# A top-k search split by batches: batches 0 and 1 searched ahead, expert 0's row groups by halves of the batches

## The chip, the cores and the metric

The kernel runs on 1 core of a Trainium2 chip. The metric is device microseconds (us) of one execution, as the median of several runs; lower is better. A profiled execution is a separate one, with its own time.

## The reference

`x` is (4, 1024, 256), the context (4, 64, 256), all in float32. A residual cross-attention comes first, then a residual mixture of 8 experts in which each expert chooses its tokens:

```python
x = x + xattn(layernorm(x), ctx, Wq, bq, Wk, bk, Wv, bv)   # scores without a scale, softmax over 64 keys
xn = layernorm(x)
probs = softmax(einsum('BTC,CE->BTE', xn, gate_w))
top_p, top_idx = top_k(transpose(probs, (0, 2, 1)), 256)    # per batch and expert, 256 of 1024 tokens
xin = xn at top_idx                                         # (4, 8, 256, 256)
h = gelu(einsum('BElC,ECH->BElH', xin, w1))                 # H = 1024
y = einsum('BElH,EHC->BElC', h, w2) * top_p
x = x + zeros.at[b, top_idx].add(y)
```

## The kernel before, in words

Each engine has its own program, written out by hand; semaphores are the only order between them. TensorE is PE, VectorE DVE, ScalarE ACT, GpSimd POOL, SyncE SP.

**Attention and gate.** The 32 chunks of 128 tokens are worked on in 8 groups of 4 (`NG`, `GT`). After a group DVE adds its attention (`x_all`, L1106) and SP stores the rows to the output. DVE and ACT make the gate's softmax `prob` in two halves, batches 0 and 1 (h=0) and batches 2 and 3 (h=1).

**Search.** The 256th largest probability of each batch and expert is found bit by bit, three bits a round, in 2 x 5 rounds (`ROUNDS`) for each half. A round of a half is a ring over two engines: DVE compares the keys with 7 candidates (`compare`, `over`, L1186, two instructions), PE counts (`count`, L872, 8 matmuls of one column), DVE tests the counts (`keep_reached`, L1192), PE turns the result into a new floor (`raise_floor`, L880), DVE makes the next candidates (`candidates`, L1197). `rounds` interleaves the two halves. Between rounds 4 and 5 the keys change from the upper to the lower 15 bits (`take_floor`, `above`, `with_lower`, `second_key`).

**First list.** For expert 0 `place_chosen(0, 0, 1)` marks the chosen tokens of all four batches and numbers them by a scan on DVE and two matmuls (`rank_bases`, L897 and L898), a one-hot product on PE (`list_expert`, L907) turns the numbers into row indices, and `index_list` writes them to `gidx`. Here a tile of 128 gathered rows holds 32 rows of each of the four batches.

**Rows in.** ACT normalises `x_all` in place (L655), SP stores it to `xn_rows` in DRAM (L447), and POOL gathers by indirect DMA, four tiles of 128 rows for each of two row groups (`gather`, L525). PE transposes the tiles (`turn`, L750), ACT rounds them (`xhi`), DVE takes the rest (`xlo`). For expert 0 the first two tiles of group 0 go ahead of the other two (`first_turn`, `first_ff1`, L994), with `keep_warm` transposes of no use before and between them.

**Expert loop.** An expert has 16 steps: 8 slices of H for row group 0, then 8 for row group 1. In a step s, PE does `ff1(s + 2)` (6 matmuls, L932) and `ff2(s)` (4 tiles, L949 and L953); ACT does the gelu (L689), DVE splits it (`split_h`, L1366 and L1368). Weights of the next expert are loaded by SP once `w2_split` shows that the raw buffers are free (L453, L454), and split by ACT and DVE from step 7 on (`w1_part`, `w1_rest`, L1374). Group 1 is turned at steps 1 and 2, the next expert's list is made at step 3 and its `gidx` at step 6, its group 0 is turned at steps 10 and 11. POOL scatters the results with an add (L533), one group after each gather. The first `ff2` of a group waits for `y_ready`, which DVE raises; for expert 0 that is a semaphore increment without work (`dve.sem_inc(y_ready, NL)`), and in the kernel before it stands ahead of `place_chosen(0, 0, 1)`. `ff1(2)` waits for the first gelu. Experts 0 to 6 run as a loop, expert 7 is written out.

Of the kernel before, what the change touches and what calls it, by code (L numbers as in the profile page):

```python
# [34 lines left out]
P = 128  # L35
# [10 lines left out]
def build(nc, x, xT, ctxT_in, Wq, WkT, Wv, WvT, bv, small, w1, w2, out):  # L46
# [33 lines left out]
    assert UB == HB and NU == 2  # L80
    assert KC == 2 and UT == 512 and B * S == 2 * P and NC * E == 256
# [8 lines left out]
    with ExitStack() as stack:  # L90
# [91 lines left out]
        own_tok = sb("own_tok", [P, NB, B], F32)  # L182
        sidx = sb("sidx", [P, NB], I32)
# [52 lines left out]
        rows_stored = sem("rows_stored")  # L236
        rows_added = sem("rows_added")
        settled = sem("settled")
        xn_stored = sem("xn_stored")
# [17 lines left out]
        all_found = sem("all_found")  # L257
        masks = sem("masks")
# [45 lines left out]
        N_CONST = 12  # L304
# [29 lines left out]
        def counts(h):  # L334

            return bank[h][:, 0:1]

        def floors(h):

            return bank[2 + h][:, 0:HB * E]  # L340

        def bases(i, n):

            return bank[2 + 2 * i][:, 0:n * 2 * B].rearrange("p (e m b) -> p e m b", e=n, m=2)
# [31 lines left out]
        def first_bank(k, rest):  # L376

            return bank[(2, 6)[k] + (1 if rest else 0)][:, 0:UF]

        def gathered_rows(g, e):  # L380

            return 16 * NL * (e + 1) - (16 * FIRST if g == 0 else 0)

# [21 lines left out]
        def _(sp):  # L405
# [23 lines left out]
            def store_rows(g):  # L429
                sp.wait_ge(x1_ready, GT * (g + 1))  # L430
                sp.dma_start(out_g[:, g // GB, g % GB], xcols(g)).then_inc(rows_stored, 16)
# [13 lines left out]
            for b in range(B):  # L445
                sp.wait_ge(xn2_ready, GB * (b + 1) + 1)
                sp.dma_start(xn_v[:, b], x_all[:, b]).then_inc(xn_stored, 16)  # L447
# [15 lines left out]
        def _(pool):  # L463
# [16 lines left out]
            pool.memset(go_on[:, :, :, :, 0:1], 0.0).then_inc(consts, 1)  # L480
            pool.iota(slot_no[:], [[1, SL], [0, TC]], base=0, channel_multiplier=0).then_inc(consts, 1)
# [55 lines left out]
            pool.wait_ge(own_set, 1)  # L537
# [5 lines left out]
            pool.wait_ge(xn_stored, 16 * B)  # L543
            pool.wait_ge(gidx_ready, 1)
            for g in range(NU):
                gather(g, FIRST if g == 0 else 0)

            def expert(e, last):
                if not last:
                    pool.wait_ge(gidx_ready, e + 2)  # L550
# [13 lines left out]
            pool.wait_ge(rows_stored, 16 * NG)  # L564
# [5 lines left out]
        def _(act):  # L570
# [76 lines left out]
            gate_exp(HALF, NC, 1)  # L647

            act.wait_ge(rows_stored, 16 * NG)
            act.wait_ge(nb2_ready, 1)  # L650

# [6 lines left out]
            for g in range(GB):  # L658
                normalise(g)
            act.wait_ge(normed, 6)  # L660
            act.activation(x_all[:, :, :, C:C + E].rearrange("p b c e -> p (b c) e"),
                           prob[:].rearrange("p b c e -> p (b c) e"), ACT.Copy).then_inc(xn2_ready, 1)
            with act.Fori(GB, NG) as g:
                normalise(g)
# [50 lines left out]
            def expert(e, last):  # L715
                for s in range(steps_of(last)):
                    if s in (1, 2):
                        x_part(1, s - 1, 2 * NU * e + 2 + s)
                    if s in (10, 11) and not last:
                        x_part(0, s - 10, 2 * NU * (e + 1) + s - 9)  # L720
# [27 lines left out]
        def _(pe):  # L748
# [136 lines left out]
            for n in range(2 * ROUNDS):  # L885
                count(0, 0, n)
                count(0, 1, n)
                raise_floor(0, n)
                count(1, 0, n)
# [3 lines left out]
            def rank_bases(i, lo, hi):  # L893
                pe.wait_ge(summed, i + 1)
                sums = upto[:, lo:hi, :, :, TC - 1]
                o = bases(i, hi - lo)
# [612 lines left out]
```

## Time and profile before

| what | us |
|---|---|
| median of 3 runs | 476.59 (476.58 to 476.61) |
| profiled execution | 479.06 |
| its span | 477.3 |
| PE busy | 445.1 (93%) |
| DVE busy | 318.0 (67%) |
| ACT busy | 212.3 (44%) |
| POOL busy | 198.2 (42%) |
| PE's mean granted clock | 0.958 of full speed |

The span runs from the first to the last instruction; the profiled time has 1.76 us more around it, and is 2.47 us above the median. Busy time of PE counts matmuls of one column and `keep_warm` transposes as well as useful ones. A time such as 83.75 below is counted from the span's start. PE's clock has two levels, 1.00 (2.4 GHz) and 0.50 (1.2 GHz).

### The profile page before, as it was taken

The numbers are of one execution on the slowest core, as the hardware profiler recorded it, in microseconds if no ns is written. First come the engines' busy times: TensorE is split into PE (matmuls) and PEld (weight loads), VectorE is DVE, ScalarE is ACT, GpSimd is POOL, SyncE is SP. The second block draws the span as 40 slices with busy tenths as digits, with TensorE's granted clock in tenths as the row PEclk, the third lists the DMA queues.
The fourth block names the chain that finished last, engine by engine and source line by source line (L and its number), as shares of the span: only waits on it lengthen the run. The fifth ranks groups of instructions, "written<-read, shape, count | busy, mean of one in ns | idle before, by whom it ended". The sixth has DMA issues, their size and how long they took to land.

```text
span 477.3 us, 8392 instructions
## 1 busy us (share of the span) xinstructions
PE 445.1 (93%) x2600; PEld 377.8 (79%) x2600; DVE 318.0 (67%) x813; ACT 212.3 (44%) x523; POOL 198.2 (42%) x222
## 2 busy tenths in 40 slices
PE   8999344899999999999999999999999999999993
PEld 7887233878888888888888888888888888888993
DVE  4788998674677467746774677467656765674551
ACT  2478697132454255424532453345234524442331
POOL 4544400600835182518252815281538153814242
PEclk9999755699999999999999999999999999999998
DMA  8984844241425251625171517150815071503142
GB/s 275 362 280 159 282 184 183 71 142 56 80 56 159 67 79 50 179 52 79 44 192 45 83 34 215 28 83 29 220 34 78 23 220 38 85 12 45 13 49 29
DMA packets 35667, 52.46 MB, mean 110 GB/s; under 512 B 3009, under 2 KB 28994, under 8 KB 35138
## 3 DMA queue, kind: packets, MB, share of 16 engines
q1 hardware_dynamic: 22946, 34.89, 21.5%
q0 software_dynamic: 12288, 17.08, 20.5%
q10 hardware_dynamic: 416, 0.27, 0.2%
q8 instruction: 9, 0.15, 0.1%
q14 instruction: 8, 0.07, 0.1%
HBM read 35.17 MB, written 16.92 MB: 109 GB/s over the span
## 4 chain that ended last, share of the span: by engine, by line
PE 88%; DVE 7%; POOL 1%; DMA 1%; ACT 1%; issue 1%; POOLq 0%; DVEq 0%
PE bank L932 37%; PE wide L949 23%; PE wide L953 12%; PE bank L750 4%; PE bank L811 3%; DVE over L1186 3%; PE wide L836 3%; PE wide L944 2%; PE bank L907 1%; DVE cand L1197 1%; DVE x_all L1106 1%; DMA wkT<-in_Wk_turned_dram 1%; PE bank L994 1%; PE wide L750 1%; DVE w1lo L1374 1%
## 5 line engine op out<-in xcount | busy, mean ns | idle before, releaser
L949 PE MATMUL wide<-w2both,hhi 128*128 128x512 f32 x480 | 176.1, 400 | 0.0
L533 POOL DMA_INDIRECT out_dram<-ysb,sidx x64 | 104.2, 1628 | 115.5 <-DVE ysb L1385 89.0
L689 ACT ACTIVATE hraw<-bank 128x512 f32<-128x512 f32 (+1 forms) x136 | 77.6, 571 | 132.5 <-PE bank L932 129.3
L953 PE MATMUL wide<-w2both,hlo 128*128 128x256 f32 x480 | 134.3, 280 | 0.0
L525 POOL DMA_INDIRECT xg<-xn_rows,gidx x64 | 65.5, 1023 | 132.5 <-issue 81.3
L1366 DVE CAST hhi<-hraw 128x512 fp32r<-128x512 f32 (+1 forms) x136 | 57.8, 425 | 80.5 <-ACT hraw L689 80.4
L949 PEld LDWEIGHTS wide<-w2both,hhi 128*128 128x128 f32 x480 | 90.5, 188 | 19.3 <-issue 0.2
L1368 DVE TENSOR_TENSOR hlo<-hraw,hhi 128x512 fp32r<-128x512 f32 (+1 forms) x136 | 90.3, 664 | 4.7
L953 PEld LDWEIGHTS wide<-w2both,hlo 128*128 128x128 f32 x480 | 90.3, 188 | 3.5
L932 PE MATMUL bank<-xhi,w1hi 128*128 128x512 f32 (+1 forms) x268 | 79.9, 379 | 0.9 <-ACT hraw L689 0.9
L932 PE MATMUL bank<-xlo,w1hi 128*128 128x512 f32 (+1 forms) x268 | 80.4, 381 | 0.0
L932 PE MATMUL bank<-xhi,w1lo 128*128 128x512 f32 (+1 forms) x268 | 80.2, 380 | 0.0
L932 PEld LDWEIGHTS bank<-xlo,w1hi 128*128 128x128 f32 x268 | 49.3, 188 | 10.3
L932 PEld LDWEIGHTS bank<-xhi,w1lo 128*128 128x128 f32 x268 | 49.3, 188 | 10.0
L932 PEld LDWEIGHTS bank<-xhi,w1hi 128*128 128x128 f32 x268 | 42.1, 188 | 6.5 <-ACT hraw L689 1.1
L682 ACT ACTIVATE xhi<-bank 128x512 fp32r<-128x512 f32 x30 | 18.0, 598 | 60.2 <-PE bank L750 60.2
L1358 DVE TENSOR_TENSOR xlo<-bank,xhi 128x512 fp32r<-128x512 f32 x30 | 20.8, 692 | 31.1 <-ACT xhi L682 29.7
L672 ACT ACTIVATE w2both<-raw 128x256 fp32r<-128x256 f32 x64 | 26.1, 417 | 26.6 <-PE wide L953 14.0
L1379 DVE TENSOR_TENSOR w2both<-raw,w2both 128x256 fp32r<-128x256 f32 x64 | 26.5, 420 | 7.5 <-ACT w2both L672 7.1
L1374 DVE TENSOR_TENSOR w1lo<-raw,w1hi 128x256 fp32r<-128x256 f32 x64 | 26.4, 422 | 0.0
L669 ACT ACTIVATE w1hi<-raw 128x256 fp32r<-128x256 f32 x64 | 25.8, 414 | 0.0
L1385 DVE SCALAR_TENSOR_TENSOR ysb<-wide,pcol,ysb 128x256 f32<-128x256 f32 x60 | 24.8, 478 | 0.0
(178 smaller groups left out, 438.6 us busy)
## 6 DMA issues: line engine op xcount, KB each, us to landing
raw<-in_w_dram SPq DMA_DIRECT2D x16, 1024.0 KB
xn_rows<-x_all SPq DMA_DIRECT2D x4, 1060.0 KB, 3.9
x_all<-in_x_dram SPq DMA_DIRECT2D x8, 512.0 KB, 9.5
raw<-in_x_turned_dram SPq DMA_DIRECT2D x8, 512.0 KB, 9.2
out_dram<-x_all SPq DMA_DIRECT2D x8, 512.0 KB, 4.8
xg<-xn_rows,gidx POOLq DMA_INDIRECT x64, 3.1
out_dram<-ysb,sidx POOLq DMA_INDIRECT x64
ctxT<-in_ctx_turned_dram ACTq DMA_DIRECT2D x1, 256.0 KB, 3.7
```

The costliest lines, as they stand in the source:

```text
L525: pool.indirect_dma_start(out=xg[g][:, i, :], out_offset=None, in_=xn_dram, in_offset=at).then_inc(first_gathered if i < first else gather ...
L533: pool.indirect_dma_start(out=out_rows, out_offset=at, in_=ysb[g][:, i, :], in_offset=None, compute_op=ALU.add).then_inc(rows_added, 16)
L669: act.activation(w1hi[:, j], w1raw[:, :, bass.ts(j, P)], ACT.Copy).then_inc(w1_hi, 1)
L672: act.activation(w2hi[:, j], w2raw[:, j], ACT.Copy).then_inc(w2_hi, 1)
L689: act.activation(hraw[s % 2][:, 0:width], bank[s % 2][:, 0:width], ACT.Gelu).then_inc(gelu_done, 1)
L932: t = pe.matmul(bank[s % 2][:, 0:width], w[:, j, k, :], xx[g][:, k, cols], start=(m == 0), stop=(m == 5))
L949: return pe.matmul(y[:, 0:2 * C], hhi[s % 4][:, at], w2both[:, j].rearrange("p a d -> p (a d)"), start=(j == 0), stop=(j == HC - 1), skip_ ...
L953: return pe.matmul(y[:, 0:C], hlo[s % 4][:, at], w2hi[:, j, :], start=False, stop=False, skip_group_check=True)
L1366: dve.tensor_copy(hhi[s % 4][:, 0:width], hraw[s % 2][:, 0:width]).then_inc(h_hi, 1)
L1368: dve.tensor_tensor(hlo[s % 4][:, 0:width], hraw[s % 2][:, 0:width], hhi[s % 4][:, 0:width].bitcast(F32), ALU.subtract).then_inc(h_split, 1)
L1374: dve.tensor_tensor(w1lo[:, j], w1raw[:, :, bass.ts(j, P)], w1hi[:, j].bitcast(F32), ALU.subtract).then_inc(w1_split, 1)
L1379: dve.tensor_tensor(w2lo[:, j], w2raw[:, j], w2hi[:, j].bitcast(F32), ALU.subtract).then_inc(w2_split, 1)
```

## The change

- Batches 0 and 1 are searched ahead: half 0 has rounds 0 to 3 nearly alone, half 1 starts beside round 3 and follows with a lag, and its rounds 5 to 9 come after half 0's list.
- Expert 0's row groups are halves of the batches: group 0 holds batches 0 and 1 (64 rows of each in a tile of 128), group 1 holds batches 2 and 3. Each group has its own mask, ranks, list and indices (`mask_rows` to `index_rows`, `rank_first`, `list_first`). Group 0 is gathered while half 1 is searched.
- PE's work on the first tiles is cut into `first_high` and `first_low`, with counts and floors of half 1 between them. 15 `keep_warm` transposes follow the first list, and twice 3.
- Group 1 of expert 0 is turned at steps 4 and 5, the list of expert 1 is made at step 6, its `gidx` at step 8, its group 0 is turned at steps 11 and 12. `mark_rest` and `place_rest` (experts 1 to 7) move into steps 1 and 3. Expert 0 is taken out of the loop and written out.
- The load of expert 1's weights also waits until group 1 is gathered.
- ACT normalises group 0's rows earlier, with the second half's exponential between, and the rows are stored under one semaphore for each half.
- POOL makes one more constant at the start (`slot_first`, 512 elements), and all engines wait for the constants.

```diff
-            with eng.Fori(0, E - 1) as e:
+            body(0, False)
+            with eng.Fori(1, E - 1) as e:
@@ next_step 11 (was 10), list_step 6 (3), index_step 8 (6), turn_step 4 (1), for expert 0 only
+        def is_first(e):
+            return isinstance(e, int) and e == 0
@@ SP
                     sp.wait_ge(w2_split, HC * (e + 1))
+                    if is_first(e):
+                        sp.wait_ge(gathered[1], gathered_rows(1, e))
@@ POOL
-            pool.wait_ge(xn_stored, 16 * B)
-            pool.wait_ge(gidx_ready, 1)
             for g in range(NU):
+                pool.wait_ge(xn_stored[g], 16 * HB)
+                pool.wait_ge(gidx_ready, g + 1)
                 gather(g, FIRST if g == 0 else 0)
@@ PE
+            for n in range(3):
+                first_half(n)
+            both_counted(3, 0)
+            both_raised(4, 0)
...
+            count(1, 0, 4)
+            rank_first(0)
+            count(1, 1, 4)
+            raise_floor(1, 4)
+            list_first(0)
+            keep_warm(bank[4], 15)
+            for n in range(5, 7):
+                second_half(n)
+                keep_warm(bank[4], 3)
...
             pe.wait_ge(first_hi, KC)
-            first_ff1(0, False)
-            first_ff1(1, False)
+            first_high(0, False)
+            first_high(1, False)
+            count(1, 0, 7)
+            count(1, 1, 7)
+            first_low(0, False)
+            first_low(1, False)
+            raise_floor(1, 7)
             pe.wait_ge(gathered[0], gathered_rows(0, 0))
             for k in range(KC):
                 first_turn(k, True)
+            second_half(8)
             pe.wait_ge(x_hi, KC)
-            first_ff1(0, True).then_inc(ff1_done, 1)
-            first_ff1(1, True).then_inc(ff1_done, 1)
+            first_high(0, True)
+            first_high(1, True)
+            first_low(0, True).then_inc(ff1_done, 1)
+            first_low(1, True).then_inc(ff1_done, 1)
+            second_half(9)
@@ PE, in the steps of expert 0
+                    if s == 0 and is_first(e):
+                        rank_first(1)
+                    if s == 1 and is_first(e):
+                        list_first(1)
+                    if s == 3 and is_first(e):
+                        rank_rest()
@@ DVE, the end of the search of half 1
+            take_floor(1, 2 * ROUNDS, last_bits)
+            whole_floor(1)
+            mask_rows(1)
+            sum_rows(1)
+            split_h(0, 0)
+            place_rows(1)
+            place_masked(1)
+            slot_rows(1)
+            block_rows(1)
+            token_rows(1)
...
             dve.sem_inc(y_ready, NL)
-            dve.wait_ge(found_ready, 1)
...
+            split_h(1, 1)
+            w2_rest(4, 4)
+            own_rows(1)
+            w2_rest(5, 5)
+            index_rows(1)
+            w2_rest(6, 6)
```

DVE, from the end of half 0's search to the first indices. Before, where all four batches are listed at once:

```order
L1223 CAST last_bits<-bank 128x16 [waits raised1]
L1392 TENSOR_TENSOR found<-found,last_bits 128x32 [waits floor_taken1,floor_taken0,found_ready]
L1298 TENSOR_TENSOR mask<-prob,found 128x32 [waits all_found]
L1298 TENSOR_TENSOR mask<-prob,found 128x32
L1309 SCALAR_TENSOR_TENSOR upto<-go_on,mask 128x64 [waits masks]
L1313 TENSOR_TENSOR place<-upto,bank 128x64 [waits ranked,summed]
```

Of the change, for batches 0 and 1 (`over` with `cand` is here half 1's round 4):

```order
L1372 CAST last_bits<-bank 128x16 [waits raised0]
L1398 TENSOR_TENSOR found<-found,last_bits 128x16 [waits floor_taken0,found_ready]
L1403 TENSOR_TENSOR mask_first<-prob,found 128x16 [waits all_found]
L1403 TENSOR_TENSOR mask_first<-prob,found 128x16
L1335 TENSOR_TENSOR over<-key,cand 128x4x112 [waits cand_ready1]
L1417 SCALAR_TENSOR_TENSOR upto_first<-go_on,mask_first 128x32 [waits first_masks]
L1335 TENSOR_TENSOR over<-key,cand 128x4x112 [waits cand_ready1]
L1423 TENSOR_TENSOR place_first<-upto_first,wide 128x32 [waits first_ranked,first_summed]
```

The same chain stands there with tiles half as large, it waits for half 0 alone, and the two comparisons of half 1 have moved in between.

DVE, around the first two splits of the gelu. Before:

```order
L1412 TENSOR_TENSOR xlo<-wide,xhi 128x256 [waits x_hi]
L1379 TENSOR_TENSOR w2both<-raw,w2both 128x256 [waits w2_hi] x3
L1366 CAST hhi<-hraw 128x512 [waits gelu_done]
L1368 TENSOR_TENSOR hlo<-hraw,hhi 128x512 [waits h_hi]
L1379 TENSOR_TENSOR w2both<-raw,w2both 128x256 [waits w2_hi] x2
```

Of the change (`sem_inc(y_ready, NL)` is no row of its own; it stands behind the second `hot_first`):

```order
L1507 CAST hhi<-hraw 128x512 [waits gelu_done]
L1509 TENSOR_TENSOR hlo<-hraw,hhi 128x512 [waits h_hi]
L1423 TENSOR_TENSOR place_first<-upto_first,bank 128x32 [waits first_ranked,first_summed]
L1429 TENSOR_TENSOR place_first<-place_first,mask_first 128x32 [waits first_placed]
L1435 SCALAR_TENSOR_TENSOR slot_any<-place_first 128x16 [waits first_placed]
L1440 TENSOR_SCALAR block_of<-slot_any 128x16 [waits first_placed]
L1442 TENSOR_SCALAR slot_of<-slot_any 128x16
L1454 TENSOR_TENSOR in_first<-block_no,block_of 128x64 [waits first_blocks]
L1447 TENSOR_TENSOR hot_first<-slot_first,slot_of 128x128x4
L1458 TENSOR_TENSOR val_first<-in_first,tok_no 128x64 [waits first_tok_found]
L1447 TENSOR_TENSOR hot_first<-slot_first,slot_of 128x128x4
L1507 CAST hhi<-hraw 128x512 [waits gelu_done]
```

Nine small instructions of the second list have moved between the two splits, and the increment of `y_ready` behind them.

PE, at the head of the steps. Of the change (before, `rank_first` is not there, and the row with `y_ready` follows the six of `ff1`):

```order
L951 MATMUL bank<-raise_by,reached 128x16 [waits reached_ready1]
L1054 MATMUL bank<-xhi,w1hi 128x512 [waits gelu_done,w1_split]
L1054 MATMUL bank<-xhi,w1hi 128x512
L1054 MATMUL bank<-xhi,w1lo 128x512 x2
L1054 MATMUL bank<-xlo,w1hi 128x512 x2
L983 MATMUL bank<-upto_first,before 128x4 [waits first_summed]
L984 MATMUL bank<-upto_first,onesb 128x2
L1071 MATMUL wide<-w2both,hhi 128x512 [waits y_ready,h_split,w2_split]
```

The last floor of half 1's search has moved directly ahead of `ff1(2)`, and the ranks of half 1 ahead of the first `ff2`.

## Rows read from the trace of the kernel before

**Rows 1.** Busy time by stretch: us, engines with (instructions), PEclk, DMA share, GB/s.
```profile
57.50:79.70 22.20, 10.98 (x172) 7.70 (x172) 20.90 (x87) 20.86 (x46) 0.00 (x0) 0.50 0.49 202
80.00:92.00 12.00, 8.30 (x46) 7.82 (x47) 9.48 (x30) 1.44 (x5) 5.58 (x5) 0.50 0.15 40
92.00:93.00 1.00, 1.00 (x9) 1.00 (x9) 0.79 (x2) 0.39 (x1) 0.69 (x2) 0.89 0.28 81
```
**Rows 2.** Waits of PE after 98 us: us in total, times, longest us.
```profile
PE bank L932 <- ACT hraw L689: 0.9, 1, 0.9
```
**Rows 3.** Timeline of the search: start us, us, engine line op out<-in xcount [idle before].
```profile
54.41 0.69 DVE L1186 TENSOR_TENSOR over<-key,first_cand 128x448 f16<-128x448 int16 x2
...
58.28 0.28 DVE L1197 TENSOR_TENSOR cand<-bank,step_bits 128x112 int16<-128x112 f32 x1
58.59 0.39 DVE L1186 TENSOR_TENSOR over<-key,cand 128x448 f16<-128x448 int16 x1
...
66.82 0.17 DVE L1223 CAST found<-bank 128x16 int32<-128x16 f32 x1
...
67.94 0.39 DVE L1186 TENSOR_TENSOR over<-key,first_cand 128x448 f16<-128x448 int16 x1
...
78.19 0.38 DVE L1186 TENSOR_TENSOR over<-key,cand 128x448 f16<-128x448 int16 x1
...
78.94 0.16 DVE L1192 TENSOR_SCALAR reached<-bank 112x1 f16<-112x1 f32 x1 [0.20 <-PE bank L872]
```
**Rows 4.** Timeline of the first list, and of what PE and DVE do behind it.
```profile
79.39 0.17 DVE L1223 CAST last_bits<-bank 128x16 int32<-128x16 f32 x1 [0.29 <-PE bank L880]
...
83.45 4.51 PE L750 MATMUL wide<-identf 128*128 128x128 f32 x20
83.75 0.27 DVE L1350 SCALAR_TENSOR_TENSOR own_tok<-bank,own_base,own 128x32 f32<-128x32 f32 x1 [0.63 <-PE bank L907]
...
84.16 2.76 DVE L1374 TENSOR_TENSOR w1lo<-raw,w1hi 128x256 fp32r<-128x256 f32 x8
```
**Rows 5.** Timeline of POOL's gathers, and how long one takes to land.
```profile
85.20 1.49 POOL L525 DMA_INDIRECT xg<-xn_rows,gidx  x1 [29.01 <-DVE gidx L1354]
...
90.04 0.95 POOL L525 DMA_INDIRECT xg<-xn_rows,gidx  x1 [0.30 <-issue]
...
118.17 0.94 POOL L525 DMA_INDIRECT xg<-xn_rows,gidx  x1 [22.18 <-DVE gidx L1354]
...
122.03 1.13 POOL L525 DMA_INDIRECT xg<-xn_rows,gidx  x1 [0.30 <-issue]
...
DMA to landing us min/median/max: 3.0/3.1/3.3
```
**Rows 6.** Timeline of PE and ACT from the first rows to the steps.
```profile
90.92 0.63 PE L750 MATMUL bank<-identf,xg 128*128 128x128 f32 x2
...
97.22 1.09 ACT L689 ACTIVATE hraw<-bank 128x512 f32<-128x512 f32 x2 [2.08 <-PE bank L994]
...
97.87 0.73 PE L932 MATMUL bank<-xhi,w1hi 128*128 128x512 f32 x2 [0.93 <-ACT hraw L689]
...
99.36 0.39 PE L949 MATMUL wide<-w2both,hhi 128*128 128x512 f32 x1
```
**Rows 7.** Timeline of expert 0's steps: the list on PE, step 7, the adds on DVE.
```profile
108.63 0.69 PE L907 MATMUL bank<-tok_val,onehot 128*128 128x32 f16 x8
...
118.98 0.62 PE L932 MATMUL bank<-xhi,w1hi 128*128 128x512 f32 x2
...
121.75 0.63 PE L932 MATMUL bank<-xhi,w1hi 128*128 128x512 f32 x2
...
122.25 1.65 DVE L1385 SCALAR_TENSOR_TENSOR ysb<-wide,pcol,ysb 128x256 f32<-128x256 f32 x4
```
**Rows 8.** Stretch of a weight load, issue to end, columns as in rows 1.
```profile
101.92:109.25 7.33, 7.33 (x47) 6.12 (x46) 5.37 (x12) 2.60 (x5) 0.00 (x0) 1.00 0.81 288
```
**Rows 9.** Timeline of DVE at the start of the kernel.
```profile
6.05 0.69 DVE L1064 TENSOR_REDUCE wq_mean<-wq_sb 128x2 f32<-128x512 f32 x1 [1.22 <-DMA wq_sb<-in_Wq_dram]
```

More of the change, by code:

```diff
@@ L657, in normalise, with keep_probabilities @@
                 a.then_inc(xn2_ready, 1)
[L658 to L663, printed above, removed]
+            def keep_probabilities(h):
+                act.wait_ge(normed, 3 * (h + 1))
+                act.activation(half(x_all, h)[:, :, :, C:C + E].rearrange("p b c e -> p (b c) e"),
+                               half(prob, h).rearrange("p b c e -> p (b c) e"), ACT.Copy).then_inc(xn2_ready, 1)
+            act.wait_ge(rows_stored[0], 16 * (NG // 2))
+            act.wait_ge(nb2_ready, 1)
+            normalise(0)
+            gate_exp(HALF, NC, 1)
+            normalise(1)
+            keep_probabilities(0)
+            normalise(2)
+            normalise(3)
+            act.wait_ge(rows_stored[1], 16 * (NG // 2))
+            act.wait_ge(nb2_ready, 2)
+            keep_probabilities(1)
+            with act.Fori(NG // 2, NG) as g:
                 normalise(g)
@@ L884, in _, with first_half @@
             pe.wait_ge(steps_set, ROUNDS + 2)
-            for n in range(2 * ROUNDS):
+            def first_half(n):
                 count(0, 0, n)
@@ new lines, in _ @@
+            lower_bits(0)
+            keep_reached(0, 4)
+            candidates(1, 1)
+            take_floor(0, ROUNDS, found)
+            above(0)
+            lower_bits(1)
+            with_lower(0)
+            compare(1, 0, 1)
+            second_key(0)
+            compare(1, 1, 1)
+            dve.wait_ge(key_ready[0], 2)
+            compare(0, 0, 5)
+            compare(0, 1, 5)
+            keep_reached(1, 1)
+            shift_found(0)
+            keep_reached(0, 5)
+            candidates(1, 2)
@@ new lines, in _ @@
+            whole_floor(0)
+            mask_rows(0)
+            compare(1, 0, 4)
+            sum_rows(0)
+            compare(1, 1, 4)
+            place_rows(0)
+            place_masked(0)
+            slot_rows(0)
+            keep_reached(1, 4)
+            block_rows(0)
+            token_rows(0)
+            take_floor(1, ROUNDS, found)
+            above(1)
+            with_lower(1)
+            dve.wait_ge(own_set, 2 + 2 * B + 3 * HB)
+            own_rows(0)
+            second_key(1)
@@ new lines, in _ @@
+            index_rows(0)
+            shift_found(1)
+            dve.wait_ge(key_ready[1], 2)
+            compare(1, 0, 5)
+            compare(1, 1, 5)
+            for j in range(6):
+                w1_rest(j, j)
+            keep_reached(1, 5)
+            w1_rest(6, 6)
+            candidates(1, 6)
+            compare(1, 0, 6)
+            compare(1, 1, 6)
+            w1_rest(7, 7)
+            keep_reached(1, 6)
+            candidates(1, 7)
+            compare(1, 0, 7)
+            compare(1, 1, 7)
@@ new lines, in _ @@
+            compare(1, 0, 8)
+            compare(1, 1, 8)
+            w2_rest(0, 0)
+            keep_reached(1, 8)
+            w2_rest(1, 1)
+            candidates(1, 9)
+            first_rest(0, True)
+            first_rest(1, True)
+            compare(1, 0, 9)
+            compare(1, 1, 9)
+            w2_rest(2, 2)
+            keep_reached(1, 9)
+            w2_rest(3, 3)
+            take_floor(1, 2 * ROUNDS, last_bits)
+            whole_floor(1)
+            mask_rows(1)
+            sum_rows(1)
```

513 lines of the change are left out of this document (319 added, 194 removed).

## The prediction, on record before the changed kernel ran

> **What bounds the kernel now.** I read the busy shares first: PE is busy for 93% of the span, DVE for 67%, so PE is the bound over the whole. Then the waits of PE after 98 us [rows 2]: there is one in all, 0.9 us, in front of the first `ff1(2)` at 97.87. From there to the end TensorE works without a gap. So whatever moves the first `ff2` (99.36, [rows 6]) moves the end by as much, and what PE does or waits for after it adds to the end in full. Ahead of it PE is not the bound: in the search, 57.5 to 79.7, DVE is busy 20.90 of 22.20 us and PE 10.98, at a granted clock of 0.50 [rows 1]. Behind the search the end hangs on a chain: the first list (79.39 on, [rows 4]), POOL's gather at 85.20 [rows 5], the first turn at 90.92, `ff1(2)`, `ff2` [rows 6]. The change works on this chain and on the first expert's steps.
>
> **Sooner: the search of half 0.** The timeline of the search [rows 3] gives the pieces of a ring: the second comparison starts 0.31 us behind the first (a pair takes 0.69), from it to the test of the counts 0.75 (78.19 to 78.94), to the new floor 0.45 (to 79.39, [rows 4]), from the candidates to the next comparison 0.31 (58.28 to 58.59). A half alone then needs 0.31 + 0.75 + 0.45 + 0.31 = 1.82 us a round, ten rounds less the last step 17.9. The change of keys takes 66.82 to 67.94, 1.12 instead of 0.31: +0.8. Half 1's comparisons from its round 0 on lie in the time in which half 0's ring waits for PE; I put what they delay at 0.6. The bounds are 0 and 2.7 (seven comparisons of 0.39 fully in the way). The first comparison, 54.41 now, has a few small gate instructions less before it: 54.0. The floor of half 0 is so taken at 54.0 + 17.9 + 0.8 + 0.6 = 73.3, now 79.39: 6.1 sooner.
>
> **The first list and gather.** From that floor to POOL's gather it is 5.81 us now (79.39 to 85.20, [rows 4, 5]), on four batches; on two the same instructions are half as wide but wait for the same partners, and two comparisons stand between. I keep 5.8: gather at 79.1. From the gather to the first turn it is 5.72 (85.20 to 90.92). PE's share of the 20 `keep_warm` was 4.51 us, 0.225 each; 15, 3 and 3 with two rounds of half 1 between end at about the same place, so I take 5.3: first turn at 84.4, 6.5 sooner (bound: 84.8).
>
> **Given back: half 1's rounds.** From the first turn to `ff1(2)` it is 6.95 us now [rows 6]. Between come rounds 7, 8 and 9 of half 1: 24 counts and 3 floors. A matmul of the search costs PE 10.98 / 172 = 0.064 us [rows 1], so 1.7, and about 0.5 of waiting for DVE in these rings. The gelu is waited for 0.93 us now, and 0.7 of it is covered by these. 6.95 + 1.7 + 0.5 − 0.7 = 8.45: `ff1(2)` at 92.85, 5.0 sooner. Four fifths of the advance are left here.
>
> **A new wait at the first `ff2`.** This is the step I put most on. `ff2(0)` waits for `y_ready`, and for expert 0 that is an increment in DVE's own order. In front of it stand now `split_h(0, 0)` and half 1's whole mask, place, slot and one-hot chain. The chain takes 79.39 to 83.12 now (the list's own wait of 0.63 and 83.75 give its end, [rows 4]), 3.7 us; `split_h` adds 1.1 (an estimate: two instructions on 128 x 512, where `w1lo` takes 2.76 / 8 = 0.35 us for 128 x 256, [rows 4]), of which 0.6 covers the wait for the ranks, which stand behind `ff1(2)` on PE; half as wide tiles give back 0.3. Half 1's last floor is directly ahead of `ff1(2)`, at 92.45: the increment comes at 92.45 + 3.9 = 96.4. PE is ready 1.49 after `ff1(2)` began, at 94.35, and waits 2.0 us. The first `ff2` starts at 96.4, not 99.36: 2.95 sooner. PE's queue is in order, so behind it waits everything that PE does; DVE's `split_h(1, 1)` stands behind the increment too, and ACT is not held. Bounds: a chain fully covered (0, start at 94.35) and one with nothing covered (0.9 more, 97.3).
>
> **Added to PE behind it.** The second list on PE costs 0.5 (8 matmuls, 0.69 with overlap, [rows 7]), the ranks of half 1 and of experts 1 to 7 apart some 0.3 more than together. These sums go to the end: +0.8. The two turns, the transposes and the list of expert 1 are moved, not added.
>
> **Group 1's rows.** Half 1's list stands in step 1, at about 99.6; from the product to the gather it is 1.45 now (83.75 to 85.20), with a `w2_rest` of `w1lo`'s size between: the gather starts at 101.3. Three tiles later (3.86 us, 118.17 to 122.03, [rows 5]) and a landing (3.1) later all are there, 108.2. A step is 2.77 us (118.98 to 121.75, [rows 7]); six `ff1` matmuls take 1.49 of it (97.87 to 99.36) and `ff2` the other 1.3, so step 4's turn comes at 96.4 + 1.3 + 3 × 2.77 + 0.8 + 1.4 = 108.2 (1.4 to 1.5 for the last `ff1`), level with the landing: I count a wait of 0.1.
>
> **Expert 1's rows.** Its indices are made at step 8, behind the adds of group 0 on DVE. These end at 122.25 + 1.65 = 123.9 now, 2.15 behind step 8's beginning at 121.75; two small instructions, and the gather starts 3.5 behind the beginning of step 8. The last tile lands 3.86 + 3.1 later, at 10.5. PE's turn, in step 11 behind six `ff1` matmuls, is due at 3 × 2.77 + 1.5 = 9.8. A wait of 0.7, where there is none now.
>
> **Weights of expert 1 later.** The load starts behind the gather, at 108.2, and takes 7.33 us (101.92 to 109.25, at 288 GB/s, [rows 8]): 115.5. It is wanted by ACT behind the gelu of step 7, whose `ff1` begins at 118.98 now and takes 1.5; 2.5 sooner that is 118.0. Room 2.5 us, so nothing; if the load were waited for, ACT's queue with gelu(10) is behind it, and it would cost what it is late. The constant more on POOL at the start is covered by DVE's wait of 1.22 us for `wq` [rows 9]; uncovered it would cost about as much as one small POOL instruction, under 0.5. The rows of each half are stored long before 79, and ACT's exponential between them is not on the chain.
>
> **Sum.** −2.95 + 0.8 + 0.1 + 0.7 = −1.35 on the profiled time of 479.06: 477.7. The profile is 2.47 above the median, so the median is 475.2.
>
> **POOL and DVE.** The first gather took 1.49 us beside `w1lo` on DVE [rows 4, 5], the later ones 0.94 to 1.13, and the four took 4.84 instead of 3.86. This is a gather slowed by DVE, by 1 us.
> The Trainium skill ("SBUF — State Buffer", section "Who interferes with whom") says that VectorE and GpSimd share a pair of ports as an exclusive lock: casts and `tensor_scalar` in their two-port modes shut GpSimd out, a `tensor_tensor` with both inputs in SBUF only keeps out GpSimd's reads. By that rule, each of the new gathers that falls beside DVE's splits is slow, and the sum would be that of the second rival below. The later gathers of the trace, which have the splits of the gelu beside them too, speak against it in part.
>
> **Rivals.**
> - *The increment costs nothing.* The chain on DVE is done before PE gets there, since `split_h` and the ranks overlap with it more than I say, or the floor comes sooner. Then the first `ff2` is at 94.35 and the sum −3.3: 473.2. For it: DVE has no other work at 92 to 97, the sum rests on three terms of my own. Against: the ranks of half 1 stand behind `ff1(2)` on PE, so that six dependent instructions (about 2.2 us) cannot start before 94.3. Chance 0.14.
> - *Slow gathers.* Both gathers of group 1 and of expert 1 take 4.84 and not 3.86: +1.0 at each turn, 475.2 + 2.0 = 477.2. Against: the rows of 118 to 122. Chance 0.14; another 0.10 for one of the two, or for one step late elsewhere, 476.2.
> - *The clock (slower than before).* The granted clock is 0.50 until 92, and 0.89 in 92 to 93, behind a stretch in which PE was busy 1.00 of 1.00 us from 91 on; in 80 to 92 PE was busy 8.30 of 12.00, with 4.5 us of `keep_warm` in one piece, and the clock did not rise [rows 1, 4]. In the changed kernel the first turns are at 84.4, but rings of half 1, in which PE waits, cut them up to 92. If the clock stays at the lower level until about 95, `ff1(2)` comes at 95.0 and `ff2`, with the same list chain before it, at 98.7: 0.7 sooner and not 2.95. With the first step partly at half clock (+0.5) that is 475.2 + 2.3 + 0.5 = 478.0. It decides from the point where the rise is behind 93. Against: 21 `keep_warm` and 40 matmuls of the search stand before the first turn, so PE is no idler than now. Chance 0.16.
>
> **How the numbers follow.** My forecast has 0.46, with its own range 474.4 to 476.2. This kernel can be told from the other by about 0.2% (1 us): faster is below 475.6, the same up to 477.5. Faster: the first rival (0.14) and 0.36 of the forecast's 0.46: 0.50. The same: 0.10 of the forecast, the 0.10 at 476.2, 0.08 of the slow gathers: 0.28. Slower: the clock 0.16 and 0.06 of the slow gathers with one more step late: 0.22. The range runs from the first rival, 473.3, to the clock's, 478.0.
>
> **What would show it.** In the profile of the changed kernel: POOL's first gather at about 79 (the search); the first turn at 84.4; `ff1(2)` at 92.9; in PE's waits one of 2 us with DVE's `y_ready` in front of the first `ff2` at 96.4; small waits for `xg` in steps 4 and 11, of 0.1 and 0.7; SP's load of expert 1 issued near 108 and over before ACT's first `w1hi` at 118; the granted clock at 1.00 from 87 to 90 on. I am wrong if the first `ff2` stands elsewhere than 95.5 to 97.5, if the waits behind it are more than 2 us, or if the clock falls or stays low beyond 92.

## The result, and the profile after

| kernel | median us (runs) | ratio to the kernel before, 95% interval |
|---|---|---|
| before | 476.58 (476.44 to 476.61) | |
| changed | 486.53 (482.69 to 490.48) | 1.017 (1.014 to 1.020) |
| changed, two later chips | 482.74 and 485.07 | 1.0103 (1.0068 to 1.0137), 1.0166 (1.0123 to 1.0209) |

I forecast 475.2 and a range up to 478.0. The kernel became slower, by 1 to 1.7%, and its runs lie far apart: nine in 478.36 to 486.38 on the second chip, where 20 of 22 of the kernel before lie in 476.61 to 479.45. The third chip has only four runs of it, 478.96, 483.78, 486.36 and 497.06, so its 1.0166 is the weakest of the three ratios. Single executions of many kernels here, that before included, take 494 us or more at a mean granted clock of 0.92 or less; the medians count them, the ratios leave them out.

The profiled execution took 490.48 us, span 488.7. Its stretches (columns as in [rows 1]):

```profile
14.00:34.00 20.00, 20.00 (x74) 16.20 (x74) 9.80 (x33) 7.77 (x28) 6.01 (x19) 0.50 0.80 268
...
89.00:92.70 3.70, 2.11 (x26) 1.33 (x24) 3.17 (x12) 0.00 (x0) 3.09 (x3) 0.96 0.23 52
92.80:99.20 6.40, 5.11 (x29) 4.46 (x29) 1.56 (x6) 0.81 (x3) 1.19 (x2) 0.50 0.18 54
99.60:105.90 6.30, 4.15 (x36) 3.33 (x34) 5.93 (x26) 2.33 (x5) 0.00 (x0) 1.00 0.00 0
106.10:109.20 3.10, 3.10 (x10) 2.62 (x11) 1.88 (x6) 0.00 (x0) 0.00 (x0) 0.51 0.00 0
```

The granted clock (1.00 or 0.50 of full speed, a mean of the two where it turns inside the stretch) is the number behind the five engines' busy times. From 14 to 34 PE worked without a pause at 0.50, in the attention, which the change does not touch. This makes the first comparison 8.4 us later than in the kernel before and is the largest part of what this execution takes longer. Shorter low stretches stand there in e1 (14.6 to 18 us), e8 (15 to 18) and e2, a kernel without the change (14.3 to 17.8). So I count from the first comparison of half 0 on. Behind it the clock goes up at 89, down at 92.5, up at 99.3, down at 106.2, up at 109.6. Its first comparison, half 0's last floor, the first turns and the first `ff1` and `ff2` of the steps:

```profile
62.85 0.69 DVE L1335 TENSOR_TENSOR over<-key,first_cand 128x448 f16<-128x448 int16 x2
...
82.12 0.17 DVE L1372 CAST last_bits<-bank 128x16 int32<-128x16 f32 x1
...
93.62 1.11 PE L821 MATMUL wide<-identf,xg 128*128 128x128 f32 x4 [1.53 <-DMA xg<-xn_rows,gidx]
...
102.63 0.70 PE L1054 MATMUL bank<-xhi,w1hi 128*128 128x512 f32 x2
...
106.06 0.65 PE L1071 MATMUL wide<-w2both,hhi 128*128 128x512 f32 x1 [1.74 <-DVEq L1707]
```

PE waits 1.53 us for the first rows, and 1.74 for `y_ready` (DVE's queue at L1707 is the increment). Both times the clock fell around the wait: inside the first (92.09 to 93.62) and just behind the second. The waits of PE after 98 us, where [rows 2] had one of 0.9:

```profile
PE wide L1071 <- DVEq L1707: 1.7, 1, 1.7
PE bank L821 <- DMA xg<-xn_rows,gidx: 1.7, 2, 1.1
PE bank L951 <- DVE reached L1341: 0.5, 2, 0.3
```

The best execution of the same kernel that a profile caught is that of e12 (478.96 us, span 477.2). There the clock is 1.00 up to 52, and the search starts at 53.68; then it is 0.50 up to 89.4 and 1.00 for good, through a wait of 1.75 us for `y_ready` too. It is the fairest match for the profiled execution of before (479.06, span 477.3), and the rows that answer to [rows 3 to 6] are:

```profile
53.68 0.69 DVE L1335 TENSOR_TENSOR over<-key,first_cand 128x448 f16<-128x448 int16 x2
...
72.92 0.17 DVE L1372 CAST last_bits<-bank 128x16 int32<-128x16 f32 x1
...
78.41 2.85 POOL L579 DMA_INDIRECT xg<-xn_rows,gidx  x1 [22.16 <-DVE gidx L1470]
...
84.56 1.12 PE L821 MATMUL wide<-identf,xg 128*128 128x128 f32 x4 [1.21 <-DMA xg<-xn_rows,gidx]
...
93.57 0.70 PE L1054 MATMUL bank<-xhi,w1hi 128*128 128x512 f32 x2
...
96.99 0.47 PE L1071 MATMUL wide<-w2both,hhi 128*128 128x512 f32 x1 [1.75 <-DVEq L1707]
```

Its stretches from the first turns to `ff1(2)`:

```profile
84.50:89.40 4.90, 4.37 (x26) 3.78 (x26) 1.01 (x3) 0.77 (x2) 0.67 (x1) 0.50 0.21 55
90.00:93.50 3.50, 2.63 (x31) 2.30 (x30) 3.47 (x13) 1.23 (x4) 0.00 (x0) 1.00 0.00 0
```

In the profile of e4, the changed kernel on the second chip (481.39 us), the clock rises at 80.6, falls at 84.1 inside a wait of 1.58 us for the first rows, and rises again at 94.3:

```profile
84.00:85.00 1.00, 0.38 (x2) 0.38 (x3) 0.00 (x0) 0.00 (x0) 0.70 (x1) 0.54 0.37 72
...
94.00:95.00 1.00, 0.74 (x12) 0.64 (x11) 0.52 (x3) 1.00 (x3) 0.00 (x0) 0.84 0.00 0
```

| place | before | forecast | e12 | e4 | e1 | profile after |
|---|---|---|---|---|---|---|
| first comparison | 54.41 | 54.0 | 53.68 | 53.78 | 55.16 | 62.85 |
| half 0's floor | 79.39 | 73.3 | 72.92 | 73.01 | 74.39 | 82.12 |
| first gather | 85.20 | 79.1 | 78.41 | 78.49 | 79.87 | 87.60 |
| first turn | 90.92 | 84.4 | 84.56 | 84.62 | 85.96 | 93.62 |
| `ff1(2)` | 97.87 | 92.85 | 93.57 | 94.80 | 95.88 | 102.63 |
| first `ff2` | 99.36 | 96.4 | 96.99 | 98.22 | 100.27 | 106.06 |
| from it to the end | 377.9 | 379.5 | 380.2 | 381.4 | 381.7 | 382.6 |

(e1 is the changed kernel with one constant made later; e9 and e15, which differ in this constant alone, have the same ratio.) From the first comparison to the first turn every execution is nearly as forecast: 30.8 to 30.9 us, where 30.4 were summed. Then they part.

### The profile page after: what moved, and what is told of

Same layout as the page of the kernel before. It is cut to its first block, busy times and chain, and to the rows that moved or that the text cites. A ratio compares the mean times of both kernels' runs of the same rounds, so it can differ in the third digit from the quotient of the medians.

```text
span 488.7 us, 8246 instructions
## 1 busy us (share of the span) xinstructions
PE 456.4 (93%) x2597; PEld 384.7 (79%) x2597; DVE 318.2 (65%) x830; ACT 212.9 (44%) x524; POOL 206.3 (42%) x230
## 4 chain that ended last, share of the span: by engine, by line
PE 71%; issue 5%; POOL 2%; DMA 2%; DVE 1%; POOLq 0%; ACT 0%
PE bank L1054 33%; PE wide L1071 21%; PE wide L1075 11%; PE bank L821 3%; PE wide L1066 2%; DMA xg<-xn_rows,gidx 2%; POOL xg L579 1%; PE bank L1029 1%; POOLq L92 0%; POOL out_dram L587 0%; DVE ysb L1521 0%; DVE hlo L1509 0%; ACT hraw L759 0%; ACT ysb L773 0%; DVE hhi L1507 0%
## 5 line engine op out<-in xcount | busy, mean ns | idle before, releaser
L587 POOL DMA_INDIRECT out_dram<-ysb,sidx x64 | 107.1, 1674 | 104.5 <-DVE ysb L1521 79.4
L579 POOL DMA_INDIRECT xg<-xn_rows,gidx x64 | 69.5, 1086 | 138.9 <-issue 99.4
L1054 PEld LDWEIGHTS bank<-xhi,w1lo 128*128 128x128 f32 x268 | 49.5, 189 | 10.1
```

The costliest lines, as they stand in the source:

```text
L579: pool.indirect_dma_start(out=xg[g][:, i, :], out_offset=None, in_=xn_dram, in_offset=at).then_inc(first_gathered if i < first else gather ...
L587: pool.indirect_dma_start(out=out_rows, out_offset=at, in_=ysb[g][:, i, :], in_offset=None, compute_op=ALU.add).then_inc(rows_added, 16)
L1054: t = pe.matmul(bank[s % 2][:, 0:width], w[:, j, k, :], xx[g][:, k, cols], start=(m == 0), stop=(m == 5))
```

## The experiments

All ratios are to the kernel before on the same chip. e1 to e3 ran together, e4 to e7, e8 to e11, and e12 to e15.

**e1: the constant made later.** In the profile after, VectorE starts 0.8 us later than before, and PE has a pause of 0.70 at 7.2; the clock falls at 14. So the first theory was the constant.

```diff
-            pool.iota(slot_first[:], ...).then_inc(consts, 1)      # ahead of slot_no
+            pool.iota(slot_first[:], ...).then_inc(steps_set, 1)   # behind first_cand
```

> The changed kernel, with the iota of slot_first (512 elements, 0.84 us) taken out of the constants that all engines wait for and put behind first_cand. Theory (start): that iota makes VectorE's first work and so kT 0.8 us later, PE waits 0.70 us at 7.2, and its granted clock falls to 0.50 from 14 to 34.5 us, which makes the search start at 62.85 and not near 54. Without it: granted clock 1.00 to 55 us, first comparison at 54.0 to 54.4, first ff2 at 96.5 to 97.5, and since from first ff2 to the end the changed kernel takes 382.6 us against 377.9, a median of 477 to 480, with runs within 1 us of each other. Rival (the low clock at 14 us is not caused by the iota): runs spread over 482 to 490 as those of the changed kernel.

Measured: 482.69 (nine runs in 478.96 to 484.5, one at 510.08), ratio 1.0072 (1.0041 to 1.0102). VectorE starts 0.8 us sooner again, but the pause of PE at 7 us is still there (0.66), and so is a fall of the clock (0.50 from 14.6 to 18), and the runs spread over 5.5 us. The theory fell. Its profile shows another low stretch, behind the search:

```profile
78.00:82.90 4.90, 4.64 (x31) 4.18 (x31) 4.60 (x18) 0.00 (x0) 2.85 (x1) 0.50 0.01 3
83.00:86.00 3.00, 1.10 (x13) 0.70 (x13) 1.82 (x6) 0.00 (x0) 2.37 (x3) 1.00 0.35 90
86.40:102.50 16.10, 13.65 (x73) 11.23 (x72) 10.05 (x36) 3.52 (x8) 0.22 (x1) 0.50 0.04 12
```

Up behind the 15 `keep_warm`; then PE is busy 1.10 of 3.00 us while it waits for VectorE and the rows; then 16 us at 0.50, in which the first turns, both first `ff1`, `ff1(2)` and the first `ff2` run.

**e2: the kernel before with such a constant.** One more iota of 512 elements into a spare tile.

> The kernel before, with one iota of 512 elements more (into a spare tile that nothing reads) among the constants that all engines wait for. Theory (start): the clock falls at about 14 us here too, and the median is 5 to 12 us above 476.6, with runs that differ by several us. Rival (start harmless, the loss comes from the search and the first steps): 476.6 to 477.4.

Measured: 478.67 (476.66 to 480.56), ratio 1.001 (0.998 to 1.004), where the kernel before has 478.44 on this chip, with 12 of its 25 runs in 478.4 to 479.5. No cost of the early constant is seen, to within the interval. The clock did fall at 14.3 in its profile, to 17.8, as it did in e1 without the early constant.

**e3: `y_ready` ahead of the list** (as e1, and:)

```diff
+            dve.sem_inc(y_ready, NL)      # behind sum_rows(1)
             split_h(0, 0)
             place_rows(1)
...
-            dve.sem_inc(y_ready, NL)      # behind token_rows(1)
```

> As e1, and the increment of y_ready moved from behind the second list's chain to ahead of split_h(0, 0). Theory: the wait of 1.7 us at the first ff2 goes, and with it the fall of the clock at 106 us, which in the changed kernel runs ff2(0) and ff1(3) at 0.50 for 3.5 us: 2 to 3.5 us less than e1. Rival (the wait is only the last of several, ranks or gelu take its place; clock falls for another reason): within 0.5 us of e1.

Measured: 480.18, ratio 1.0030 (1.0007 to 1.0052), 2.0 us below e1 by the ratios, but their intervals overlap. In its profile the wait for `y_ready` is gone, with 0.6 us at the same instruction left that nothing in the profile names; from `ff1(2)` to the first `ff2` it takes 2.3 us, where e12 and e4 take 3.4. That profile is of an execution of 495.81 us with the clock at 0.50 from 29 to 107, so it cannot show whether the fall behind the wait is gone too.

**e4: the changed kernel again.**

> The changed kernel again, on the same chip as the next three. The kernel with the constant made later had runs of 479 to 484.5 us. Theory (the constant costs nothing; the loss is the granted clock from the first rows to the first steps, 86 to 102 us, and 3.8 us behind the first ff2): 479 to 484.5 again. Rival (the constant early costs several us by itself): 3 us or more above the kernel of e1, its fastest run over 481.

Measured: 482.74 (478.36 to 486.38), ratio 1.0103 (1.0068 to 1.0137). About the spread of e1, as the first theory of the two said; the rival, with no run under 481, fell.

**e5: `keep_warm` until the rows come** (as e3, 12 for 3 behind round 6).

> As e3 (y_ready early), and 12 instead of 3 keep_warm transposes behind half 1's round 6, so that PE is busy while it waits for the first rows (1.5 us idle there in e1, after which its granted clock fell from 1.00 to 0.50 and stayed there for 16 us). Theory (the fall costs 4 to 5 us, since ff1, ff2 and the turns to 102 run at half clock): granted clock 1.00 through the first turns, first turn to first ff2 in 10 to 10.5 us instead of 14.3, median 3 to 4.5 us below e3 (near 476). Rival (the fall is not from this gap, or the chain there is VectorE's and not PE's): within 1 us of e3, the clock low behind the first turns all the same.

Measured: 477.59, ratio 0.9995 (0.9976 to 1.0015), eight of ten runs in 475.96 to 478.39 and two at 486.12 and 487.61. Against 1.0103 for e4 that is 5.1 us less, for both edits together. Against e3, by its ratio on another chip, it is 1.7 us, where 3 to 4.5 were expected, and the intervals overlap. The clock did not behave as expected in the profiled execution: it still fell at 83.4 and rose at 90.2, not at 94 as in e4. PE had been busy 0.74, 0.53 and 0.74 in the microseconds from 80 to 83, in the rings of rounds 5 and 6, where no more transposes were added.

```profile
83.00:84.00 1.00, 1.00 (x9) 0.96 (x7) 0.73 (x2) 0.00 (x0) 0.95 (x1) 0.72 0.50 127
...
90.00:91.00 1.00, 0.85 (x11) 0.42 (x9) 0.99 (x4) 0.76 (x2) 0.00 (x0) 0.87 0.00 0
```

The same kernel on another chip, e11 below, did something else: the clock stayed at 0.50 up to 85.6 and rose for good.

```profile
84.00:85.00 1.00, 1.00 (x6) 1.00 (x5) 0.09 (x1) 0.00 (x0) 0.70 (x2) 0.50 0.15 59
85.00:86.00 1.00, 1.00 (x8) 0.90 (x6) 0.00 (x0) 0.05 (x1) 0.56 (x1) 0.69 0.52 136
```

From the first turn to `ff1(2)` it took 9.01 us in e5 and 7.27 in e11. So one execution does not tell what the clock does in a kernel.

**e6: `w1_rest` behind the rounds** (as e3, VectorE's eight `w1_rest` moved behind the comparisons of round 7).

> As e3, and VectorE's eight w1_rest moved from before and between rounds 5 to 7 of half 1 to behind them, so that nothing of them runs beside POOL's first gather (2.85 us in e1, 1.49 in the kernel before). Theory (VectorE's tensor_tensor of two SBUF inputs slows POOL): first gather under 1.6 us, first turn 1.3 us sooner relative to the floor of half 0. Rival (the gather is slow for another reason): still 2.8.

Measured: 478.68, ratio 1.001 (0.9988 to 1.0033), not to be told from e3. The first gather of e3, then that of e6:

```profile
96.47 2.85 POOL L579 DMA_INDIRECT xg<-xn_rows,gidx  x1 [23.02 <-DVE gidx L1470]
```

```profile
96.38 1.25 POOL L579 DMA_INDIRECT xg<-xn_rows,gidx  x1 [23.04 <-DVE gidx L1470]
```

1.6 us shorter, and the first turn came 4.74 us behind the gather's start instead of 6.15. Both profiled executions took 495 us; among those of 475 to 478 us e5 has 2.85 again and e10 below, with the edit of e6, 1.25. So the gather is short when the subtractions are away. But they are not enough to make it slow: in e15, which leaves them where e3 has them, six of them run beside it and it took 1.51 (these two are rows of e15):

```profile
96.29 2.09 DVE L1358 TENSOR_TENSOR w1lo<-raw,w1hi 128x256 fp32r<-128x256 f32 x6
96.64 1.51 POOL L579 DMA_INDIRECT xg<-xn_rows,gidx  x1 [23.04 <-DVE gidx L1471]
```

The Trainium skill ("SBUF — State Buffer", section "Who interferes with whom") says that a VectorE instruction with two inputs in SBUF contends with a GpSimd instruction that reads SBUF; `w1lo` is such an instruction. The pair e3 and e6 is in line with it, if the gather counts as such a read, which no run here shows; why e15 (1.51) and the kernel before (1.49, [rows 5]) lost so little in the same company, neither the section nor a run here explains.

**e7: the kernel before without its 34 `keep_warm`.**

> The kernel before without its 34 keep_warm transposes (20, 8 and 6) between the first list and the first ff1. Theory (the granted clock after the first list is worth microseconds in this place): the clock stays at 0.50 beyond 92, to 96 or more, and the time is 1.5 to 4 us above the kernel before. Rival (the clock rises with the first rows anyhow): within 0.5 us.

Measured: 478.58 (478.03 to 478.97), ratio 1.0031 (1.0018 to 1.0045): 1.5 us. Its clock:

```profile
88.00:93.00 5.00, 3.42 (x15) 2.83 (x16) 2.80 (x8) 0.77 (x2) 3.86 (x4) 0.50 0.40 109
93.00:94.00 1.00, 1.00 (x7) 1.00 (x7) 0.00 (x0) 0.00 (x0) 0.92 (x1) 0.52 0.51 123
94.00:98.00 4.00, 3.47 (x22) 2.78 (x20) 3.06 (x8) 2.16 (x5) 0.97 (x2) 1.00 0.27 72
```

Even with none, it rises at 94 and stays up. That kernel gives PE its turns and `ff1` in one piece, which the change took away; that this is why it rises is likely, but no run tests it, and in e4 the clock rose at 94.3 as well.

**e8 to e11, on one chip.** e8 is e5 with `return 7 if is_first(e)` for 8 in `index_step`; e9 is e8 with 7 `keep_warm` for 3 behind round 5 and 3 behind the first turns; e10 is e9 with `w1_rest` as in e6; e11 is e5 again.

> As e5, and expert 1's indices made at step 7 and not 8, so ahead of the four adds on VectorE and one step sooner. Theory: the wait for expert 1's rows, 1.2 us at step 11 (4.42 us from ff1 to ff1 in place of 3.22 in e5), goes, 1.2 us below e5. Rival (the gather then collides with VectorE's adds and splits and is as late, or the list is not ready on PE): within 0.3 us of e5.

> As e8, and 7 instead of 3 keep_warm behind round 5, and 3 between the first turns and the first ff1. In e5 the granted clock rose at 80.0 but fell again at 83.7 for 6.6 us, after 3.4 us in which PE was busy 0.74, 0.53, 0.74 of each us. Theory (the idle time of PE in the two rings makes it fall): clock 1.00 from 80 on without a break, first turn to first ff2 in 9.5 instead of 11.3 us, 1 to 1.8 us below e8, and the runs closer together. Rival (VectorE's ring, not PE, sets that stretch; or the added transposes make PE late in the ring): within 0.4 us of e8 or slower.

> As e9, and w1_rest behind the rounds as in e6: the first gather takes 1.5 and not 3.15 us with its gap, the first turn is 1.4 us sooner, and first ff2 0.6 to 1.2 sooner, median the same below e9: near 473, 3.5 us below the kernel before. Rival (w1_rest then delays the first ff1's xlo): within 0.3 us of e9.

> The kernel of e5 again, as the measure for the other three on this chip: 476 to 477.7 as before.

| kernel | median us | ratio, 95% interval |
|---|---|---|
| e11 (e5 again) | 476.88 | 1.0002 (0.9975 to 1.0029) |
| e8 | 475.70 | 0.9969 (0.9956 to 0.9982) |
| e9 | 474.92 | 0.9954 (0.9939 to 0.9969) |
| e10 | 475.06 | 0.9960 (0.9941 to 0.9978) |

The step at which expert 1's rows are turned takes 4.52 us in e12, of which 1.09 are the wait; in e8 3.21. In e12 it looks so:

```profile
128.75 0.62 PE L1054 MATMUL bank<-xhi,w1hi 128*128 128x512 f32 x2
...
131.38 0.66 PE L821 MATMUL bank<-identf,xg 128*128 128x128 f32 x4 [1.09 <-DMA xg<-xn_rows,gidx]
...
133.27 0.39 PE L1054 MATMUL bank<-xhi,w1hi 128*128 128x512 f32 x1
```

In e8:

```profile
127.65 0.62 PE L1054 MATMUL bank<-xhi,w1hi 128*128 128x512 f32 x2
...
130.86 0.63 PE L1054 MATMUL bank<-xhi,w1hi 128*128 128x512 f32 x2
```

e8's median is 1.2 us below e11's, as expected, and the step is shorter by as much; the ratios' intervals just overlap. e9 is a further 0.8 lower, a little less than expected and not clear of e8's interval; seven of its ten runs lie in 474.4 to 475.2 and two at 494. Its profile is of one of these two, so the clock between 80 and 94 is to be read from e10, where it no longer falls:

```profile
81.00:93.90 12.90, 10.62 (x98) 8.79 (x96) 11.27 (x40) 2.71 (x7) 2.08 (x2) 1.00 0.12 32
```

But e10 is no faster than e9: my expectation of 0.6 to 1.2 us was wrong. The first gather takes 1.25 there too, but the first turn comes 5.37 us behind its start, with no wait for rows before it: PE reaches it late, behind its own added transposes and VectorE's rounds. The first rows are no longer what is waited for. The rival, within 0.3 us of e9, came true, though not for the reason it gave.

**e12 to e15, on one chip.** e12 is the changed kernel again, e13 moves only `y_ready` (as e3), e14 adds only the `keep_warm` (as e9), e15 is e9 with the constant where the change has it.

> The changed kernel, as the measure for the next three on this chip: 478.5 to 486, ratio to the kernel before 1.010 to 1.017.

> The changed kernel with nothing but the increment of y_ready moved ahead of split_h(0, 0). If the wait at the first ff2 costs what its size and the steps at half clock behind it say: 2 us below e12. If it only shifts the wait to another place: under 0.7.

> The changed kernel with nothing but more keep_warm in the rings and before the first rows (7 and 12 for 3 and 3, and 3 behind the first turns). If the granted clock in 84 to 95 is the larger part of the loss: 2.5 to 4 us below e12, the runs closer together. If not: under 1 us.

> The kernel of e9 with slot_first among the constants again, as in the changed kernel. If the early constant costs nothing, a ratio of 0.995 to 0.997 as e9 had (474.9). If it delays the start by its 0.8 us or makes the clock fall at 14 us more often: 0.8 us or more above that, 0.998 and over.

| kernel | median us | ratio, 95% interval |
|---|---|---|
| e12 changed | 485.07 | 1.0166 (1.0123 to 1.0209) |
| e13 only `y_ready` | 479.51 | 1.0042 (1.0021 to 1.0064) |
| e14 only `keep_warm` | 477.10 | 1.0015 (0.9997 to 1.0034) |
| e15 all but the constant | 475.09 | 0.9954 (0.9937 to 0.9971) |

By the ratios `y_ready` alone gives back 5.9 us and the 16 more `keep_warm` (13 in the rings, three behind the turns) 7.2, where I had expected 2.5 to 4; eight of e14's ten runs lie in 476.7 to 477.3. Both figures hang on e12's four runs, of which the two lowest alone average 481.4, 1.009 of the kernel before. Measured from e4's ratio of 1.0103 they are 2.9 and 4.2, and e3 against e1 gave 2.0 for `y_ready`. So the transposes are worth 4 to 7 us, clear of the noise against e4 and e12; `y_ready` is worth 2 to 6 us, and whether that is more than the length of its wait is not settled. All edits together give 10.1 us from e12 and 7.1 from e4. The single gains, with 1.2 for the index step, sum to 14.3 and 8.3. Whether `y_ready` and the transposes share a part of the loss is open too. The profiles of e13 and e15 are of executions of 498.67 and 494.14 us, with the clock at 0.50 from 29 to 117.3 and 104.3, so only those of e12 and e14 show what it does behind 80. e15 has the ratio of e9, so no cost of the early constant is seen. The first turn, `ff1(2)` and the clock between them in e14:

```profile
84.40 0.66 PE L821 MATMUL wide<-identf,xg 128*128 128x128 f32 x4 [0.60 <-DMA xg<-xn_rows,gidx]
...
91.62 0.70 PE L1054 MATMUL bank<-xhi,w1hi 128*128 128x512 f32 x2
```

```profile
84.40:91.60 7.20, 6.13 (x62) 5.25 (x63) 4.83 (x17) 2.09 (x6) 0.61 (x1) 1.00 0.14 38
91.60:95.10 3.50, 1.76 (x10) 1.24 (x10) 3.16 (x16) 1.22 (x3) 0.00 (x0) 1.00 0.01 2
```

7.2 us in place of 9.0 in e12 and in the profile after, 10.2 in e4 and 9.9 in e1, for the same work and three transposes more. Here the clock rose at 81.2. The wait for `y_ready` is still 1.7 us here, and the clock stays up through it.

## Why the prediction was wrong

- **The search, the first list, the gather: right.** 73.3, 79.1 and 84.4 were forecast; e12 has 72.92, 78.41 and 84.56. Two errors cancel in the last: the gather began 0.7 sooner than summed, and from it to the first turn it took 6.15 and not 5.3, with a first gather of 2.85 us.
- **The step that failed: TensorE's clock, first of all in "Given back: half 1's rounds", 8.45 us from the first turn to `ff1(2)`.** It starts from the 6.95 us of the kernel before, of which all but 1.3 ran at 1.00, and expects the higher clock from 87 to 90 on; no term of the sum has a second fall. Measured: 9.0 in the best execution, 9.9 to 10.2 in e1 and e4; with the clock at 1.00 throughout 7.2 (e14). The work was even overestimated; its speed was wrong. The change cuts PE's one dense piece of work into pieces with rings of VectorE and a wait for rows between them. In e12 the clock did not rise before 89.4; in e1, e4 and the profile after the rise that followed the 15 `keep_warm` was lost again at the first rows (86.3, 84.1 and 92.5), and in the last once more behind the wait for `y_ready`.
The Trainium skill ("TensorE: Matmul & The Clock Gate", section "What's actually happening") says that the activity window behind the gate is free-running and does not start with the kernel, so where the clock turns varies from run to run. The profiles agree in kind: for one kernel, e5 had its rise near 80, a fall at 83.4 and a rise at 90.2, e11 a single rise at 85.6.
- **What each term cost.** Against the 477.7 summed for a profiled execution, e12 is 1.3 us longer, e4 3.7, the profile after 12.8. From the first turn to `ff1(2)` lie 0.6, 1.7 and 0.6 of this, behind the first `ff2` 0.7, 1.9 and 3.1. The profile after has 8.9 more ahead of the first comparison, where the sum only took off 0.4. So the 8.45 by itself explains the smaller part of the miss; the clock, low at other places in other executions, explains most of it in the profile after.
- **The clock rival had the mechanism and was mis-sized.** It put `ff1(2)` at 95.0 and the first `ff2` at 98.7; e4 has 94.80 and 98.22, and its 481.39 is not far from the 480.5 that 478.0 stands for in a profiled execution. But I let the clock rise once at 95 for good. In e1 it was low from 86.3 to 103.3, through the first `ff2` (100.27) and `ff1(3)`; in the profile after it fell again at 106.2. I gave it 0.16 and 478.0 as its time; medians were 482.7 to 486.5.
- **From the profile to the median: wrong.** I took 2.47 us off because the profiled execution of before lay that far above its median, and nothing showed that the surplus would be there in the changed kernel's profile and not in its median. Without this step the forecast is 477.7. Even e12's lowest run, the one profiled, was 478.96. Where the surplus lies no run shows: no execution of the kernel before at 476.6 was traced. The granted clock alone hardly explains it, 0.958 against 0.959 to 0.962 in runs at 476.5 to 477, and on e1's chip 12 of that kernel's 25 runs lie at 478.4 to 479.5, with the same clocks of 0.957 to 0.961.
- **The new wait at `ff2`: right** (2.0 forecast, 1.75 measured), first `ff2` 96.4 against 96.99. Whether it costs more than its length is open: taking it away was worth 2.0 us in e3 and 2.9 to 5.9 in e13, and three of the five executions with the wait whose profiles were taken show no fall of the clock behind it (e4, e12, e14); in e1 the clock was low already. The rival in which the increment costs nothing fell. (Its sum is −3.4 by the terms given, not −3.3; this changes nothing.)
- **The steps behind: nearly right.** +1.6 forecast, +2.3 in e12. Expert 1's rows were waited for 1.09 us, not 0.7; the first of its gathers took 1.40. Group 1's 0.1 us was right in e12, where no wait is seen, but in e4 it was 0.85. The second rival did not come true: from the first to the fourth start the gathers of group 1 took 4.1 us and those of expert 1 4.6, against 3.86 counted and 4.84 in the rival. The gather that was much slower, the very first, was not in it.
- **Weights later: right in cost, wrong in detail.** In e12 the load was issued at 109.15 and ACT did wait for it, which I had not expected, but PE shows no wait for it:

```profile
117.28 0.42 ACT L739 ACTIVATE w1hi<-raw 128x256 fp32r<-128x256 f32 x1 [0.88 <-DMA raw<-in_w_dram]
```

**What stays open.** No profile caught an execution of the changed kernel between 482 and 488 us without a low clock ahead of 34 us too. So how much of the loss of such a run lies in the falls behind 80, and how much in an early one, is not measured in one execution; that e13 and e14, which differ from e12 only behind 80, bring the runs that are compared down to 480.2 and less shows that most of it hangs on what stands there. Why then early falls would be rarer in them is not explained; with four to ten runs of each it may be chance.

The versions that beat both kernels most are e9 and e15: 0.9954 of the kernel before, 2.2 us less. That their 474.9 and 475.1 lie near my 475.2 is luck: these kernels have neither the wait for `y_ready` nor the one for expert 1's rows, which my sum counted at 2.0 and 0.7, and my sum took off 2.47 for which no run gives a reason.

## What to carry to other kernels

A change that starts a dense stretch of TensorE sooner by cutting it into pieces has to be priced at both clock levels, and a pause in it can cost more than its length; adding transposes of no use to the rings and around the first turns was worth 4 to 7 us here. Ask of an increment without work what now stands ahead of it in its queue. A profiled execution's surplus over the median may belong to that execution alone, and may not be subtracted from another kernel's sum before it is known what it is.

## What the runs showed of the hardware

- The granted clock fell in or just behind a wait of PE of 1.5 to 1.7 us and then stayed at 0.50 for 3 to 17 us (e1, e4, the profile after), in e1 even with PE busy 13.65 of 16.10 us. It did not fall at waits of 1.7 to 1.8 us for `y_ready` in e4, e12 and e14, and in e5 it fell at 83.4 with PE busy, behind three microseconds of 0.74, 0.53 and 0.74. The length of one wait does not decide it.
- Two executions of one kernel had the clock turn at different places: near 80, 83.4 and 90.2 us in e5, 85.6 alone in e11.
- A GpSimd indirect DMA of 128 rows took 2.85 us beside VectorE subtractions of two SBUF inputs in e3, e5, e9 and e12 and 1.25 without them in e6 and e10, but 1.49 and 1.51 beside them in the kernel before and in e15.
- Without any `keep_warm` the kernel before loses 1.5 us only; 16 more of them in the changed kernel were worth 4 to 7.
